# Attention kernel on one core: row maxima of two heads split on VectorE, the guard of the division without a product, the loop dealt anew

## What is computed

```python
h = jnp.maximum(_layernorm(x, axis=-1), 0.0)
msg = h_neigh[None, :, :] + E[edge_types]
q = (h_target @ Wq.T + bq).reshape(Bt, H, DH)
k = (msg @ Wk.T + bk).reshape(Bt, Bn, H, DH)
v = (msg @ Wv.T + bv).reshape(Bt, Bn, H, DH)
scores = jnp.einsum('bhd,bnhd->bhn', q, k) / np.sqrt(DH).astype(np.float32)
scores = jnp.where(mask, jnp.float32(-1000000000.0), scores)
attn = jax.nn.softmax(scores, axis=-1)
attn = jnp.where(mask, jnp.float32(0.0), attn)
out = jnp.einsum('bhn,bnhd->bhd', attn, v).reshape(Bt, d)
return x + out @ Wo.T + bo
```

## Time and profile before

| | |
|---|---|
| median of three runs | 49.84 us |
| the profiled execution's own time | 49.53 us |
| its span, first to last instruction | 47.7 us |
| DVE busy | 39.1 us, 82% |
| PE busy | 42.2 us, 88% |
| ACT busy | 33.6 us, 70% |
| POOL busy | 30.0 us, 63% |
| 32 maxima on DVE (L476) | 19.9 us, idle before them 0.5 us |
| granted TensorE clock | 1.000 |

### The profile page before, as it was taken

How to read it: one execution, slowest core, us unless ns; L and a number is a source line. 1 busy time by engine, 2 the same in 40 slices (tenths; PEclk the granted TensorE clock), 3 DMA queues, 4 the chain that set the end, 5 groups by cost and what they waited for, 6 DMA issues and landing times.

```text
span 47.7 us, 834 instructions
## 1 busy us (share of the span) xinstructions
PE 42.2 (88%) x253; PEld 17.9 (37%) x256; DVE 39.1 (82%) x110; ACT 33.6 (70%) x60; POOL 30.0 (63%) x53
## 2 busy tenths in 40 slices
PE   0799996889997999999999999999999999999800
PEld 0323234365325244244544352252412233476500
DVE  2694696786898999999999999899788969999400
ACT  0293528689998759999999999599759999200410
POOL 5881005089996999484858579990899999800000
DMA  0499998980099999910000000000000000000032
GB/s 0 81 317 449 399 311 180 406 376 22 0 215 194 192 283 206 204 31 0 0 0 0 7 0 7 0 0 14 0 0 0 0 0 0 0 14 0 0 139 81
DMA packets 2071, 4.93 MB, mean 103 GB/s; under 512 B 258, under 2 KB 786, under 8 KB 1810
## 3 DMA queue, kind: packets, MB, share of 16 engines
q1 hardware_dynamic: 1490, 2.38, 21.2%
q10 hardware_dynamic: 576, 2.49, 13.9%
HBM read 3.02 MB, written 0.26 MB: 69 GB/s over the span
## 4 chain that ended last, share of the span: by engine, by line
PE 65%; DVE 17%; ACT 9%; issue 3%; DVEq 0%
PE ps L655 15%; PE ps L622 10%; PE ps L547 8%; PE ps L672 8%; PE ps L610 7%; DVE masked_scores L476 4%; PE ps L630 4%; PE ps L650 3%; ACT prob L395 3%; DVE turned_U L502 3%; DVE scaled L506 3%; DVE masked_n L491 3%; PE ps L556 2%; DVE ctxT L515 2%; PE ps L578 1%
## 5 line engine op out<-in xcount | busy, mean ns | idle before, releaser
L476 DVE CUSTOM_DVE_ANT_0 masked_scores<-ps,mask_b 128x512 bf16<-128x512 f32 x32 | 19.9, 687 | 0.5 <-PE ps L610 0.3
L260 POOL TENSOR_TENSOR prob<-prob,live 128x512 int32<-128x512 int32 x11 | 13.9, 1279 | 0.0
L395 ACT ACTIVATE prob<-ps 128x512 f32<-128x512 f32 x23 | 12.2, 599 | 1.0 <-PE ps L655 0.8
L655 PE MATMUL ps<-stack 98*128 98x512 bf16 x32 | 11.0, 381 | 0.3 <-issue 0.2
L622 PE MATMUL ps<-stack 96*128 96x512 bf16 x28 | 9.8, 379 | 0.4 <-DMA stack<-split 0.3
L491 DVE TENSOR_TENSOR masked_n<-ps,veto 128x512 f32<-128x512 f32 x9 | 5.7, 684 | 1.0 <-PE ps L655 1.0
L395 ACT ACTIVATE prob<-masked_n 128x512 f32<-128x512 f32 x9 | 5.2, 624 | 1.0 <-DVE masked_n L491 1.0
L236 POOL COPY split<-split 128x512 int32<-128x512 int32 (+1 forms) x4 | 1.9, 508 | 5.4 <-ACT split L333 3.9
L547 PE MATMUL ps<-ones 128*128 128x512 bf16 x9 | 4.0, 628 | 1.4 <-DVE ones L414 1.4
L655 PEld LDWEIGHTS ps<-stack 98*128 98x128 bf16 x32 | 3.1, 97 | 5.2 <-ACT stack L366 1.3
L366 ACT ACTIVATE stack<-ps 2x512 bf16<-2x512 f32 x8 | 4.7, 590 | 0.4
(11 more groups left out here) (73 smaller groups left out, 56.7 us busy)
## 6 DMA issues: line engine op xcount, KB each, us to landing
stack<-split SPq DMA_DIRECT2D x8, 192.0 KB, 4.0
adj_b_sb<-adj_b_dram ACTq DMA_DIRECT2D x1, 1024.0 KB, 7.1
adj_n_sb<-adj_n_dram ACTq DMA_DIRECT2D x1, 1024.0 KB, 10.0
pk<-pack_k_dram ACTq DMA_DIRECT2D x1, 322.0 KB, 3.7
xt<-x_dram SPq DMA_DIRECT2D x1, 256.0 KB, 3.5
pw<-pack_w_dram SPq DMA_DIRECT2D x1, 192.0 KB, 4.9
out_dram<-y SPq DMA_DIRECT2D x1, 192.0 KB, 1.9
brow<-bias_rows_dram SPq DMA_DIRECT2D x1, 128.0 KB, 8.3
```

Source lines behind the costliest of these rows:

```text
L260: nc.gpsimd.tensor_tensor(bits, bits, live[:, LIVE_TILES.index(t), :], ALU.mult).then_inc(cut_done, 1)
L395: nc.scalar.activation(prob[:, h, t, :], scores, ACT.Exp, scale=DH ** -0.5).then_inc(exp_done, 1)
L476: nc.vector.tensor_tensor_reduce(out=masked_scores[:, k % len(A_BANKS), :], in0=ps[:, A_BANKS[k % len(A_BANKS)], :], in1=mask_b[:, t, :], ...
L655: nc.tensor.matmul(bank, stack[0:rows_of(h), h, SIDE["k"], t * P:(t + 1) * P], stack[0:rows_of(h), h, SIDE["q"], :], start=(h, t) not in O ...
```

## The change

`split_max` of heads 0 and 7 goes from POOL to DVE, straight behind these heads' last maxima (`SPLIT_BY_VECTOR`), with semaphores of its own; POOL keeps the six others. `add_tiny` and its constants go: the first product into each accumulator starts it, and the division's multiplication becomes one instruction that takes the smaller of the reciprocal and 1e30 before multiplying. There are eight products of ones instead of nine. In the front, PE takes the first key part away between the two halves of the query projection, the first two products for V come ahead of the first query part, and DVE makes all its masks before the first maximum. In the loop, the tables of who masks what, where turns, products with V and A tiles stand, are dealt anew; all of DVE's nine masked subtractions come after the last maximum, and the output bias on POOL comes ahead of the last two cuts.

```diff
-WARM_UP = 9
+WARM_UP = 8
-ON_DVE = [ORDER[18]] + [ORDER[24]] + [ORDER[23]] + ORDER[25:29] + ORDER[30:32]
+ON_DVE = ORDER[22:29] + ORDER[30:32]
-TURN_AT = ((0, 7), (3, 11), (6, 15), (10, 19), (14, 23), (18, 27), (22, 32), (25, 32))
+TURN_AT = ((0, 7), (3, 11), (6, 15), (10, 20), (15, 25), (16, 28), (21, 32), (24, 32))
+SPLIT_BY_VECTOR = (0, 7)
-PLACED_AT = {1: 2, 2: 5, 3: 9, 4: 13, 5: 17, 6: 20, 7: 22}
+PLACED_AT = {1: 2, 2: 5, 3: 9, 4: 13, 5: 15, 6: 21, 7: 21}
...
             make_live(1)
-            split_max(0)
             make_live(3)
             split_max(1)
...
+            def split_max(h):
+                dve.wait_ge(max_found, (h + 1) * BT)
+                if h == 0:
+                    dve.wait_ge(max_parts_zero, 1)
+                high, low = (max_parts[:, h, :, PAIR_ROWS + row] for row in range(MAX_ROWS))
+                nc.vector.tensor_copy(high, row_max[:, h, :]).then_inc(ends_high, 1)
+                dve.wait_ge(ends_high, SPLIT_BY_VECTOR.index(h) + 1)
+                nc.vector.tensor_tensor(low, row_max[:, h, :], high, ALU.subtract).then_inc(ends_split, 1)
...
-                nc.vector.tensor_tensor(
-                    scaled[:, blocks, g * DH:(g + 1) * DH], turned_U[:, g, blocks, 0:DH],
+                nc.vector.scalar_tensor_tensor(
+                    scaled[:, blocks, g * DH:(g + 1) * DH],
                     recip[:, g, blocks].rearrange("p (k c) -> p k c", c=1).to_broadcast([P, tiles * P // CT, DH]),
-                    ALU.mult).then_inc(u_scaled, 1)
+                    MOST, turned_U[:, g, blocks, 0:DH], ALU.min, ALU.mult).then_inc(u_scaled, 1)
...
+            project_q(0)
             take_k_away(0)
+            project_q(1)
+            project_v((0, 1))
             take_q_away(0, (0,))
-            project_v((0, 1))
```

More of the change, by code:

```diff
@@ L23 @@
 FLOOR = -(2.0**29)
-TINY = 1e-30
+MOST = 1e30
 EPS = 1e-5
@@ L243, in make_live @@
                                         ALU.is_equal, ALU.is_equal).then_inc(live_ready, 1)
-            def split_max(turn):
-                heads = slice(TURNS[turn][0], TURNS[turn][-1] + 1)
-                pool.wait_ge(max_found, heads.stop * BT)
-                if turn == 0:
+            def split_max(h):
+                pool.wait_ge(max_found, (h + 1) * BT)
+                if h == 1:
                     pool.wait_ge(max_parts_zero, 1)
-                end = PAIR_ROWS + MAX_ROWS * len(TURNS[turn])
-                high, low = (max_parts[:, turn, :, PAIR_ROWS + row:end:MAX_ROWS].rearrange("p t h -> p h t")
-                             for row in range(MAX_ROWS))
-                nc.gpsimd.tensor_copy(high, row_max[:, heads, :]).then_inc(high_ready, 1)
-                pool.wait_ge(high_ready, turn + 1)
-                nc.gpsimd.tensor_tensor(low, row_max[:, heads, :], high, ALU.subtract).then_inc(max_split, 1)
+                high, low = (max_parts[:, h, :, PAIR_ROWS + row] for row in range(MAX_ROWS))
+                nc.gpsimd.tensor_copy(high, row_max[:, h, :]).then_inc(high_ready, 1)
+                pool.wait_ge(high_ready, h)
+                nc.gpsimd.tensor_tensor(low, row_max[:, h, :], high, ALU.subtract).then_inc(max_split, 1)
             def cut(h, t):
@@ L297, in _ @@
             split_max(3)
-            cut(1, 1)
-            split_max(4)
-            pool.wait_ge(live_ready, 2)
-            cut(1, 3)
-            split_max(5)
-            cut(0, 3)
+            pool.wait_ge(live_ready, 2)
+            cut(0, 3)
+            cut(2, 1)
+            split_max(4)
+            cut(2, 3)
+            split_max(5)
+            cut(1, 3)
+            cut(1, 1)
+            split_max(6)
             cut(3, 3)
-            split_max(6)
-            cut(2, 3)
-            split_max(7)
+            cut(5, 1)
             cut(3, 1)
-            cut(2, 1)
-            cut(5, 1)
+            add_out_bias()
             cut(4, 1)
             cut(4, 3)
-            add_out_bias()
         @block.scalar
@@ L547, in _ @@
                 nc.tensor.matmul(ps[:, WARM_BANK, :], ones[:, 0:P], ones[:, :], start=True, stop=True)
-            def add_tiny(bank, columns):
-                pe.wait_ge(tiny_set, 1)
-                nc.tensor.matmul(ps[:, bank, 0:columns], tiny_row[0:1, :], ones[0:1, 0:columns], start=True, stop=False,
-                                 skip_group_check=True)
-            add_tiny(ACC_BANK, B)
             pe.wait_ge(msg_ready, 1)
@@ L590, in _, with project_q @@
             pe.wait_ge(pw_loaded, 16)
-            for i in range(HALVES):
+            def project_q(i):
                 pe.wait_ge(hT_ready[i], 1)
@@ L625, in turn_max @@
             def turn_max(turn):
-                pe.wait_ge(max_split, turn + 1)
+                if turn in SPLIT_BY_VECTOR:
+                    pe.wait_ge(ends_split, SPLIT_BY_VECTOR.index(turn) + 1)
+                else:
+                    pe.wait_ge(max_split, turn)
                 if turn >= 1:
@@ L682, in last_product_with_v @@
                     last = nc.tensor.matmul(ps[j * CT:(j + 1) * CT, TAIL_ACC[i], 0:tiles * P], V[:, t, HG + j, :],
-                                            prob[:, HG + j, t, first * P:(first + tiles) * P], start=False,
-                                            stop=t == V_LAST[i][-1], tile_position=(0, j * CT), skip_group_check=True)
+                                            prob[:, HG + j, t, first * P:(first + tiles) * P],
+                                            start=t == V_LAST[i][0], stop=t == V_LAST[i][-1], tile_position=(0, j * CT), skip_group_check=True)
                 if t == V_LAST[i][-1]:
@@ L728, in score_places @@
                     score_by_neighbour(k)
-            score_places(0, 26)
+            score_places(0, 27)
             pe.wait_ge(max_found, H * BT)
-            for i in range(len(PIECES)):
-                add_tiny(TAIL_ACC[i], PIECES[i][1] * P)
-            score_places(27, 31)
+            score_places(28, 30)
             last_product_with_v(0, 0)
+            score_places(31, 31)
             last_product_with_v(0, 1)
```

45 lines of the change are left out of this document (21 added, 24 removed).

## The result

The changed kernel takes 51.45 us (median of 4, 51.17 to 52.07) beside 49.93 us of the kernel before (4 runs): ratio 1.032, 95% interval 1.027 to 1.038. It is slower by 3.2%; 49.4 us was forecast, with 50.2 us as the upper end.

A forecast was written before the change was run, and what follows sets the result against it. DVE's line of work from 14.66 us on was taken to set the end; front, head 0's split, loop, subtractions and end put the transpose 0.5 earlier, less 0.05: -0.45 us, median 49.4, range 48.9 to 50.2.

The forecast's parts named there:

- The second rival: Loop gain eaten: second veto falls into POOL's cut of (5,1), 0.5 us, or A tile 26/head 5 late; 49.85, chance 0.17.
- The first rival: POOL's `live` for tile 3 holds the subtraction in head 0's split on DVE, up to 1.25 us; 50.65, chance 0.13.
- Split of head 0: Between fourth and fifth maximum on DVE: two dependent small instructions cost +0.35 us, bounds 0.2 and 0.46, nothing hiding them.
- Front: Ahead of the maxima: keys start earlier, 0.3 us taken; head-0 scores gain 0.1 to 0.2: -0.15 (ends 0 and -0.5).
- Loop: During the maxima on DVE: tile 18's subtraction leaves, -0.60; the stall of 0.17 and 0.04 behind it goes, -0.20.
- the place that was called tight: In the loop: A tile 26 ready at about 28.95, DVE asks at 29.0, no slack; 0.05 allowed for tight places.
- "-0.5" at the end: Behind the last exponential: DVE free at 41.05, first piece's transpose starts at 41.35 instead of 41.87, -0.5 us.
- Time outside the span: Execution time beyond the profiled span: the forecast carried over 1.83 us from the kernel before.
- the division: At the end: POOL adds the output bias earlier, done near 39.6, so the first `scaled` takes 0.43 instead of 0.77.
- the minimum at the price of the plain product: In the division: the product with the minimum should cost as much as the plain one.
- no wait on POOL's turned heads: In the loop: POOL's splits of heads 3, 4 and 5 are turned one or two A tiles later, so PE does not wait.
- ACT not the bound: At the end: ACT's exponentials end at 40.4 to 40.5, before 40.82; as close a bound as DVE's, giving back 0.1.

The follow-up runs named there:

- new front alone: Kernel before with only the changed order of the front, masks included; nine products of ones and add_tiny stay: 50.02 us beside 49.61, ratio 1.005.
- nine ones (new order): Changed kernel with POOL waiting for the vetoes before its cut of (5,1), head 0's split on POOL and nine products of ones: 50.03 us, ratio 1.0089.
- two more writes on VectorE (old order): Best kernel (front of before, cut of (3,1) ahead of (5,1), tile 31 first) plus two idle writes on DVE: 49.29 us, ratio 0.9935.
- the wait: Changed kernel with POOL waiting for both odd vetoes before its cut of tile (5,1), nothing else: 50.98 us beside 49.81, ratio 1.0248.
- two idle writes: Two unread POOL writes behind its last cut, added to the kernel with POOL's wait, front of before and head 0's split on DVE: 50.36 us, ratio 1.0114 (without: 1.0267).
- hold-alone kernel: Changed kernel with head 0's split on POOL, front of before and nine ones, but no POOL wait before the cut of (5,1): 50.85 us, ratio 1.0247.
- loop-alone kernel: Changed kernel with POOL waiting for the vetoes, head 0's split on POOL, front of before and nine ones: 49.71 us beside 49.69, ratio 1.0002.
- split 0 on GpSimd: Changed kernel with GpSimd waiting for the vetoes and splitting head 0 again; eight ones and new front stay: 50.14 us, ratio 1.007.
- the same with tile 31 first: Changed kernel with GpSimd waiting for vetoes and splitting head 0, plus tile 31's scores ahead of the last group's first products: 50.1 us, ratio 1.0068.

## Why the prediction was wrong, step by step

*The hold of the veto: the step that failed most.* The second rival named the place and the mechanism (the second veto in POOL's cut of (5,1), from 33.15; it came at 33.85), but gave it 0.5 us and a share of 0.17. The sum of the forecast had nothing for it. It is 1.07 at the vetoes, 0.68 where the late B tiles have taken their part back, and 0.8 in the time. The veto waits until an instruction that began first has ended, so the price is what is left of the cut: by the forecast's own places (second veto about 0.34 behind 33.05, cut from 33.15, 1.28 long) some 1.0 us, not 0.5. Of DVE instructions in a 2-port mode the Trainium skill (SBUF — State Buffer, "Who interferes with whom") says that whoever issues first gets the shared port pair for its whole instruction and the other fully blocks. The trace agrees for the veto (0.42 becomes 1.50 beside a cut of 1.42), though no row says in which mode it ran, and the forecast had cited that section for another place.

*The first rival did not happen.* In the middle of POOL's two `live` the subtraction of head 0's split took 0.18, and the cast 0.28 (0.25 to 0.29 in the six other kernels with that split) instead of 0.18. With the earlier trace rows this says that POOL's instructions with one input (`live`, the mask) hold DVE little here, and those with two (cut, bias) hold it to their end; why, no run shows. The same section of the Trainium skill says that a DVE instruction with two SBUF inputs contends with a GpSimd instruction that reads SBUF, and `live` reads it; here the subtraction with two inputs was not held by it. The measurement decides.

*Split of head 0: 0.35 forecast, 0.52 in the rows, 0.56 in the time.* The upper bound (0.46) did not hold: from the reading to the cast 0.12, from the cast to the subtraction 0.32 (0.1 of it the slower cast), and 0.08 to the maximum. Head 7's, where POOL was at rest, took 0.12 + 0.21 + 0.08 = 0.41 against 0.35.

*Front: -0.15 forecast, +0.25 us measured.* The sign was wrong. The step that failed is the second half of the queries "seen by DVE at about 9.05, before at 9.16": it took no account of what the new order costs. From the start of `k_head` to DVE's work on that half it is 1.45 us in the kernel before and 1.80 in after (1.80 with the new front alone), with DVE waiting for PE's product of that half (0.66, before 0.31), and the fp32 scores of head 0 follow with the same 0.35: 3.21 us behind `k_head` before, 3.56 in after. Of the 0.37 that the keys start earlier, 0.14 is left at `k_head`, so the scores come 0.21 later and the fourth maximum 0.22. Where `k_head` comes early, the order costs less: with nine ones (new order) and with two more writes on VectorE (old order) it starts at 7.52 and 7.51, DVE gets the second half at 9.40 and 9.19, and the fourth maximum starts at 14.90 and 14.69, 0.21 apart. In the time, the new order alone costs 0.25 (1.005 in the kernel before), and taking it out of others gives 0.3 and 0.43. In the profiled execution `pk` also landed 0.27 later than before, which shifts all of this alike.

*Loop: -0.60 and -0.20 forecast, and these came.* From the fifth maximum to the last it is 16.69 us, 16.62 forecast (17.42 before, less 0.80), with DVE standing still once, for 0.11 at the place that was called tight (29.53 to 29.64). The rest of the end failed in size: the forecast had the first to the last subtraction at 5.15, it was 5.45 in after, with 0.41 for tile 31, and where the hold is taken away the late B tiles take 0.68 (0.27 + 0.41). So of the 0.68 us that the forecast won between the fifth maximum and the transpose (25.87 against 26.55) nothing is left even without the hold: it is 26.72 to 26.74. The "-0.5" at the end (0.48, since the transpose of before starts at 41.83, not 41.87) counted DVE and tile 31, but not that the cut of (3,1) is behind (5,1), nor that PE's products behind the last exponential are the next bound 0.3 us further.

*Time outside the span: taken as unchanged, +0.32 us.* Nothing in the profile of before could have told this, since it is one number there.

*Right:* the division (0.43, `scaled` no longer held), the minimum at the price of the plain product, no wait on POOL's turned heads, ACT not the bound.

*Together, in the rows.* The two profiled executions (51.45 and 49.53 us) differ in four stretches: up to the fourth maximum +0.22, from there to the fifth +0.51, from the fifth maximum to the transpose of the first piece +0.85 (27.40 and 26.55), from the last issue to the end +0.34. That is 1.92, the whole difference; from that transpose to the last issue both take 4.11. Of the 0.85, 0.68 is the hold; the other 0.18 is the new deal of the loop with the split of head 7, which the forecast had at -0.68.

*In the time* the sum is looser: hold 0.8, split 0 0.56, front 0.25, tail 0.34, in all 1.95, beside 1.60 us measured with a remainder that is neutral (1.0002). The removals one after another give 0.37 for the wait (0.49 with equal tails), 0.89 for split 0 with its tail, 0.34 for the front and the ninth one; these add up to 1.60 by the way they are made. Each step is good to 0.3 to 0.5 us, which covers the difference; whether the hold is worth less in the time while the other causes stand is open. In the rows it is not: 0.68 with them, 0.67 without.

## What to carry to other kernels

An instruction that another engine can hold is priced by what is left of the holder, up to its whole length, so before vetoes, casts or small sums of SBUF data are moved, look for what the other engine has open at that moment, and let it wait or put it elsewhere. Work moved onto the engine that is full costs its full hand-over, 0.4 to 0.5 us for two instructions on 4 elements. Compare the time with the span in every run: a difference between them that is constant within a kernel and changes between kernels is a cause like any other; look at the stretch behind the last issue too, since part of it can lie inside the span. Time won on one engine late in a kernel is kept only up to the next engine's line of work; look at that one first.

## What the hardware showed that was not expected

The end of an execution has two levels here, 3.6 and 4.0 us behind the last issue, and GpSimd's program decides: two idle writes there bring it from 4.07 to 3.60, and the hold-alone kernel, one GpSimd wait shorter than the loop-alone kernel, has 3.97 where that has 3.58. In after the guard's two writes and two splits left GpSimd (53 to 47 instructions), which put it on the long side. What goes with it in all 20 traces is the third instruction packet on q14: with 53 instructions on GpSimd it comes at 29 to 30 us, with 51 at 35, with 49 and the wait at 41 to 43, and with 49 without it or 47 only behind the output, where the end is 0.4 later. (The page's table counts packets inside the span alone.) The two idle writes bring the packet from 49.4 back to 42.4 us and the end with it. That q14 brings GpSimd's instructions is inferred from this; why the execution's end waits for the packet is not shown.

The keys' product took 1.12 to 2.08 us in the profiled executions, with the granted clock at 1.00 from 5 to 8 us in all. Two kernels with one and the same front (split 0 on GpSimd; the same with tile 31 first) took 2.08 and 1.22, so start times in the front of single executions cannot be set against each other, only distances from one row to another and the medians of many executions.
